# A two-layer network on one core: the last sums of the second layer put into the next pair's turn, its opening run sequence by sequence, and the router's silu computed through the tangent

## The reference, cut to what matters

```
x = x + attn0(cond0(x))
h = cond2_0(x)            # layer norms, an MLP with silu, layer norm
x = x + experts(h)        # softmax router, top 2 of 8, 80 slots per sequence
x = x + attn1(cond1(x))
x = x + ffn1(cond2_1(x))
```

```
out = acc * x_scale * weight_scale + bias      # then added to x
```

## Time and profile before

| | us |
|---|---|
| median of 3 runs | 2380.55 (2374.33 to 2380.96) |
| the profiled execution's own time | 2381.17 |
| its span | 2379.4 |

### The profile page before, as it was taken

How to read it: one execution, slowest core, us unless ns; L and a number is a source line. 1 busy time by engine, 2 the same in 40 slices (tenths; PEclk the granted TensorE clock), 3 DMA queues, 4 the chain that set the end, 5 groups by cost and what they waited for, 6 DMA issues and landing times. The chain is left out here.

```text
span 2379.4 us, 33839 instructions
## 1 busy us (share of the span) xinstructions
PE 2054.9 (86%) x11838; PEld 1300.9 (55%) x11838; DVE 1314.7 (55%) x3682; ACT 1019.4 (43%) x2518; POOL 862.2 (36%) x594
## 2 busy tenths in 40 slices
PE   5588898898898898898898898899999497979897
PEld 4355554554555555555555555567788254545555
DVE  3757577577577577577577544512111255655545
ACT  2244466466465465466466456331222041414141
POOL 1717265365364364364364320411000341515131
PEclk9586999988988988988988889799999698999998
DMA  7000110210210210210210220333454411202000
GB/s 279 36 21 1 52 49 1 92 27 1 92 27 1 92 27 1 92 27 1 92 27 1 81 72 1 125 119 121 150 188 144 143 40 35 56 18 72 18 14 19
DMA packets 67429, 145.89 MB, mean 61 GB/s; under 512 B 16356, under 2 KB 42074, under 8 KB 62946
## 3 DMA queue, kind: packets, MB, share of 16 engines
q1 hardware_dynamic: 51434, 93.79, 11.7%
q0 software_dynamic: 15872, 50.35, 7.3%
HBM read 114.64 MB, written 29.46 MB: 61 GB/s over the span
## 5 line engine op out<-in xcount | busy, mean ns | idle before, releaser
L1386 ACT ACTIVATE att_buf<-att_buf,nmin 128x384 f32<-128x384 f32 (+3 forms) x512 | 288.6, 564 | 402.8 <-DVE nmin L1751 402.6
L1164 PE MATMUL bank<-kk,qT 32*128 32x512 f32 (+2 forms) x1024 | 292.6, 615 | 39.0 <-DVE nmin L1751 38.7
L1197 PE MATMUL bank<-ident,att_buf 128*128 128x128 f32 x1280 | 227.7, 306 | 58.9 <-ACT att_buf L1394 58.2
L901 POOL TENSOR_TENSOR big<-ex_at,kx 128x2048 f32<-128x2048 f32 x56 | 206.8, 3720 | 163.4 <-DVE xt_na L1496 130.1
L1740 DVE TENSOR_TENSOR att_buf<-bank,wdiag 128x128 f32<-128x128 f32 x384 | 93.0, 284 | 241.7 <-PE bank L1169 240.4
L1394 ACT COPY att_buf<-bank 128x384 f32<-128x384 f32 (+3 forms) x512 | 211.0, 412 | 28.7 <-PE bank L1211 27.0
L1211 PE MATMUL bank<-att_buf,vp 128*32 128x128 f32 x2560 | 219.0, 308 | 0.0
L1197 PEld LDWEIGHTS bank<-ident,att_buf 128*128 128x128 f32 x1280 | 158.2, 157 | 79.1 <-ACT att_buf L1386 77.2
L913 POOL DMA_INDIRECT buf_d<-nB,sidx x64 | 62.6, 978 | 358.2 <-DVE sidx L1615 341.1
L1211 PEld LDWEIGHTS bank<-att_buf,vp 128*32 128x32 f32 x2560 | 136.0, 121 | 55.1 <-issue 47.4
L1164 PEld LDWEIGHTS bank<-kk,qT 32*128 32x128 f32 x1024 | 100.5, 205 | 117.5 <-DVE nmin L1751 64.8
(11 more groups left out here) (377 smaller groups left out, 4097.5 us busy)
## 6 DMA issues: line engine op xcount, KB each, us to landing
big<-in_eW SPq DMA_DIRECT2D x16, 1024.0 KB, 7.9
kk<-in_eW SPq DMA_DIRECT2D x16, 1024.0 KB, 7.7
buf_d<-zero SPq DMA_DIRECT2D x8, 640.0 KB, 7.5
xt_na<-in_xT SPq DMA_DIRECT2D x8, 512.0 KB, 3.5
nA<-in_xN SPq DMA_DIRECT2D x8, 512.0 KB, 3.6
x_d<-x SPq DMA_DIRECT2D x8, 512.0 KB, 3.3
x<-x_d SPq DMA_DIRECT2D x8, 512.0 KB, 4.3
out<-qf SPq DMA_DIRECT2D x8, 512.0 KB, 2.9
```

The lines of the kernel that those rows point to most:

```text
L901: pool.tensor_tensor(pv[:, c * P:(c + 1) * P, :].rearrange("p (h d) o -> p o h d", d=DH), spread(ex[:, t, :, 8 * c:8 * c + 8], 3, DH), spr ...
L1164: pe.matmul(bank[u % 2][:, 0:n], qT[r:r + 32, g, i * P:(i + 1) * P], kk[r:r + 32, g, T * i * P:T * i * P + n], start=True, stop=False)
L1197: mm = pe.transpose(bank[3 + u % 2][:, j * P:(j + 1) * P], pr[:, u % NPR, j * P:(j + 1) * P], ident[:])
L1386: act.activation(pr[:, u % NPR, 0:n], pr[:, u % NPR, 0:n], ACT.Exp, scale=-1.0, bias=nmin[:, u % 4:u % 4 + 1], accum_out=rsum[:, i, h:h + ...
```

## The change

1. **Router's activation.** silu(v) = v * (0.5 * tanh(0.5 v) + 0.5) with v = u + b. ScalarE: two `Tanh` with scale 0.5 and bias `half_b`, then two `Identity` with scale 0.5 and bias 0.5 in place. VectorE, at a new step "gate" (unit 26, 27 in the last pass): two `scalar_tensor_tensor` (bank + bias) * aT3, which now raise `u_ok`. VectorE prepares `half` and `half_b` once in each pass.
2. **Last sums of a turn.** `finish` (the same five instructions for each lane) stands at stage `ST_IN` of the next turn; SyncE stores from there. Only the last turn also finishes itself. So that the banks are free, `QK_OUT` becomes (0, 1, 2, 3, 0, 1), and TensorE waits for the lane's four sums before it writes bank 2. GpSimd's new `xb` waits for the lane's finish, and ScalarE's first write to `qf` for the store's landing. `gi` is fetched at the turn's start, and `row_numbers` stands behind kT and k2 on VectorE. Turn 0 is now written out ahead of the loop.
3. **Opening.** TensorE and ScalarE do the whole head of lane 0, then of lane 1. VectorE waits for the two head weights alone, prepares both heads' weights, then does `combine` lane by lane; its preparation of the turn's weights (`wqb`, `orfk`, `orfq`) comes last.

```
-def body(b2, more):
+def finish(dve, v, s, name):
+    for t in range(T):
+        dve.scalar_tensor_tensor(fo[:, t, :], bk[2 + t // 2][...], ab[:, 1, t:t + 1], row("ws"), ALU.mult, ALU.mult).then_inc(s(name + "_raw"), 1)
+    dve.wait_ge(s(name + "_raw"), T)
+    dve.tensor_tensor(fo, fo, v["xb"][:], ALU.add).then_inc(s(name), 1)
+def body(b2, before, more):
...
 sync:
+    if more: fetch_gates(...)            # both lanes, first of all
     brow, wde loads
+    if before: store(..., "fin0", LANES * b2 - LANES + n)
     if more: wait xb_ok; fetch_rows; fetch_head
-    wait fin; store; wait out
+    if not more: store(..., "fin", ...)
...
 gpsimd:
+    if before: pool.wait_ge(s("fin0"), 1)
     pool.tensor_tensor(v["xb"][:], v["x2"], ..., ALU.add)
...
 tensor:
+    if before and i == 2: pe.wait_ge(s("fin0_raw"), T)
...
 vector:
+    if before:
+        yield ST_IN
+        finish(dve, v, s, "fin0")
     yield ST_QK
-    if more: row_numbers(dve, v, s)
     kT, k2
+    if more: row_numbers(dve, v, s)
...
-with nc.Fori(0, B // LANES - 1, hint_back_edge=True) as b2:
-    body(b2, True)
-body(B // LANES - 1, False)
+body(0, False, True)
+with nc.Fori(1, B // LANES - 1, hint_back_edge=True) as b2:
+    body(b2, True, True)
+body(B // LANES - 1, True, False)
```

More of the change, by code:

```diff
@@ L676, in program @@
                 pc3 = sb("pc3", [P, 8])
+                half_b = sb("half_b", [P, K2])
+                half = sb("half", [P, 1])
                 gac = sb("gac", [P, T, 2 * D])
@@ L1325, in router_stream @@
                                     out_of_bank(3)
+                                    yield AT["silu"]
+                                    act.wait_ge(s("half_ok"), 2)
                                     for o in range(K2):
-                                        yield AT["silu"]
                                         act.wait_ge(s("u_mm"), o + 1)
-                                        act.activation(aT3[:, o, :], bank[SIDE[o]][:], ACT.Silu, bias=pc3[:, 6 + o:7 + o]).then_inc(s("u_ok"), 1)
+                                        act.activation(aT3[:, o, :], bank[SIDE[o]][:], ACT.Tanh, bias=half_b[:, o:o + 1], scale=0.5)\
+                                            .then_inc(s("tanh_ok"), 1)
+                                    for o in range(K2):
+                                        act.wait_ge(s("tanh_ok"), o + 1)
+                                        act.activation(aT3[:, o, :], aT3[:, o, :], ACT.Identity, bias=half[:, 0:1], scale=0.5).then_inc(s("gate_ok"), 1)
                                     yield AT["sd3"]
@@ L1553, in router_stream @@
                                     yield from affine(nB, nB[:], gb[:, :, 0:D], gb[:, :, D:2 * D], AT["h2b"], "h_ok")
+                                    yield AT["gate"]
+                                    for o in range(K2):
+                                        dve.wait_ge(s("gate_ok"), o + 1)
+                                        dve.scalar_tensor_tensor(aT3[:, o, :], bank[SIDE[o]][:], pc3[:, 6 + o:7 + o], aT3[:, o, :],
+                                                                 ALU.add, ALU.mult).then_inc(s("u_ok"), 1)
                                     yield AT["y_in"]
@@ L1860, in layer1, with in_stages @@
             lane_bufs.append(v)
-        def in_stages(s, *programs):
-            live = [p(n, lane_bufs[n], lambda name, n=n: s(f"{name}_{n}")) for p in programs for n in range(LANES)]
+        def in_stages(s, *programs, lanes=None):
+            lanes = range(LANES) if lanes is None else lanes
+            live = [p(n, lane_bufs[n], lambda name, n=n: s(f"{name}_{n}")) for p in programs for n in lanes]
             due = [next(g) for g in live]
@@ L2028, in _ @@
                     def _(sp):
+                        if more:
+                            for n, v in enumerate(lane_bufs):
+                                fetch_gates(sp, v, lambda name, n=n: s(f"{name}_{n}"), LANES * b2 + LANES + n)
                         for n, v in enumerate(lane_bufs):
@@ L2039, in _ @@
                                 fetch_head(sp, v, lambda name, n=n: s(f"{name}_{n}"), LANES * b2 + LANES + n)
-                        for n, v in enumerate(lane_bufs):
-                            sp.wait_ge(s(f"fin_{n}"), 1)
-                            sp.dma_start(out[LANES * b2 + n].rearrange("(t p) d -> p t d", p=P), v["fo"]).then_inc(s(f"out_{n}"), 16)
-                        for n in range(LANES):
-                            sp.wait_ge(s(f"out_{n}"), 16)
+                        if before:
+                            for n in range(LANES):
+                                sp.wait_ge(s(f"fin0_out_{n}"), 16)
+                        if not more:
+                            for n, v in enumerate(lane_bufs):
+                                store(sp, v, lambda name, n=n: s(f"{name}_{n}"), "fin", LANES * b2 + n)
+                            for n in range(LANES):
+                                sp.wait_ge(s(f"fin_out_{n}"), 16)
                     @block.gpsimd
@@ L2095, in lane @@
                                     pe.wait_ge(s("ksq_ok"), 2 * (i - 3))
+                                if before and i == 2:
+                                    pe.wait_ge(s("fin0_raw"), T)
                                 for m in range(K2):
@@ L2310, in lane @@
                             dve.wait_ge(s("acc_mm"), 1)
-                            for t in range(T):
-                                done(dve.scalar_tensor_tensor(fo[:, t, :], bk[2 + t // 2][:, (t % 2) * D:(t % 2 + 1) * D], ab[:, 1, t:t + 1],
-                                                              row("ws"), ALU.mult, ALU.mult))
-                            settle()
                             dve.wait_ge(s("x3b_ok"), 1)
-                            dve.tensor_tensor(fo, fo, v["xb"][:], ALU.add).then_inc(s("fin"), 1)
+                            if not more:
+                                finish(dve, v, s, "fin")
                         in_stages(s, lane, *([head_dve(dve)] if more else []))
                 s.clear()
-        with nc.Fori(0, B // LANES - 1, hint_back_edge=True) as b2:
-            body(b2, True)
-        body(B // LANES - 1, False)
+        body(0, False, True)
+        with nc.Fori(1, B // LANES - 1, hint_back_edge=True) as b2:
+            body(b2, True, True)
+        body(B // LANES - 1, True, False)
 def layouts(i):
```

51 lines of the change are left out of this document (37 added, 14 removed).

## The result

The changed kernel took 2303.28 us (median of 4 runs, 2299.39 to 2307.12), the kernel before beside it 2377.44 us: a ratio of 0.969, 95% interval 0.9661 to 0.9719. The rival that came nearest is the one in which the clock comes back too (2315). In every table behind this the medians are over all executions, while the ratios and intervals leave out the slow ones, those over 1.5% above the fastest of their kernel.

A forecast was written before the change was run, and what follows sets the result against it. TensorE's stops and clock were taken to bound the kernel. Router 17.5, last pass -2.0, opening 7.1 and gaps 25.5 summed to 48.1 us off 2381.2, giving 2333.1 profiled and 2332 us forecast; range 2313 to 2353.

The forecast's parts named there:

- the one in which the clock comes back too: Rival: the high clock returns at the router and at the turns, 65.5 us gained, 2315 us; chance 0.15.
- Step 1, the sure part: Router, seven passes: ScalarE free 1.3 us earlier, TensorE's 2.50 us stop becomes 1.2 us; 9 us gained.
- Step 1, the clock: Router, seven passes: shorter stop may keep TensorE's clock up, up to 2.4 us more a pass, half counted.
- The gate at nothing: Router, seven passes: VectorE's two added gates, about 1.65 us, cost nothing; cover is some 1 us.
- Its rival (2350): Router: VectorE's delayed biases give back the 1.3 us and the clock; 2350 us, chance 0.2.
- Step 2: Router, last pass: halvings and gate delay the `wint2` matmuls, 2 us lost, up to 4 with the clock.
- Step 3: Opening: turn 0 starts on TensorE at 1886.7 instead of 1893.83, 7.1 us gained, ends 5 and 9.
- Step 4: Three gaps between turns: stop falls to 2.5 us, 8.5 us a gap, 25.5 us gained, ends 16 and 28.
- The clock behind it, counted at nothing: Turn starts after the shortened gaps: 2.9 us a turn hang on the clock; nothing counted, 9 us as good end.
- The rival in which work comes back inside the turn: Turns: VectorE's sums and later gathers delay TensorE at lane 1's values; 2340 to 2344 us, chance 0.08.

The follow-up runs named there:

- first pair of traces: Profiled executions of the first comparison: the kernel before at 2381.17 us and the changed kernel at 2299.39 us.
- group 3: One chip, the changed kernel and three variants with TensorE's router stop at 0.88, 2.10, 2.50, 2.71 us: 2382.24, 2390.68, 2420.14, 2414.65 us.
- hold 2: Changed kernel plus two unread ScalarE activations behind the halvings in the seven attention passes: 2390.68 us against the changed kernel's 2382.24 in group 3.
- silu passes: Changed kernel with silu back in the seven attention passes, tangent and gate only in the last: 2420.14 us against the changed kernel's 2382.24.
- Silu last: Changed kernel with silu kept in layer 0's last pass only: 2377.49 us against the changed kernel's 2384.88 in group 4; 2355.19 us in group 1.
- group 4: One chip: before 2438.95 us, changed 2384.88, seven passes' halving on VectorE with silu in the last 2356.16, silu last 2377.49, router as before 2423.44.
- the gaps alone: Changed kernel with the last sums and stores put back into their own turn: 2396.62 us against the changed kernel's 2374.3.
- all of layer 1: Changed kernel with the router as before: 2383.09 us against the kernel before's 2402.04 in group 1; ratio 0.9965 in group 4.
- group 1: One chip: before 2402.04 us; changed kernel with router as before 2383.09, router's change alone 2372.08, silu last 2355.19, hold 2 2364.92.
- group 5: One chip: kernel before profiled again, 2370.27 us against 2373.29; changed kernel with seven passes' halving on VectorE and silu in the last, 2292.31 us.
- groups 2 to 4: Follow-ups on one chip each; the first of them had before 2434.92 us, changed 2374.3, three unread activations 2418.06, halving on VectorE 2367.34, sums put back 2396.62.

## Why the prediction was wrong

*What bounds the kernel.* That TensorE's stops and its clock are what counts held everywhere.

*Step 1, the sure part:* right in kind, a little low. ScalarE saved 1.50 us where 1.3 were forecast, since tangents, halvings and the exponential overlap by 0.12 us at each seam; the stop shrank by 1.62. That is 7 x 1.62 = 11.3 us against 9. By the 2.66 us a switch of the Trainium skill ("ScalarE: Activation LUTs", What ACT_TABLE_LOAD costs) two switches would, as an estimate, have been worth 5.3 us, and 4 us after the halvings. The rows show 1.50: two loads of 1.28 us less the halvings' 1.34, and 0.3 us at the seams. The measurement decides, and no drain is in it.

*Step 1, the clock: this is the step that failed.* I had "up to 2.4 us more a pass ... I count half of it", that is 1.2. The first pair of traces has 43.5 / 7 = 6.2 us of busy time a pass, and group 3 has 27 us beyond the stop's length, 3.8 a pass. Two things were wrong. I priced only the matmuls that stand behind the stop, and the clock is lost and won in the whole rest of the pass: of the 43.5 us only 10.5 lie between the first and the last `wint2` matmul. And "Neither row says whether a stop of 1.2 us does so; I count half of it" put a chance into a sum: the rival in which it comes back had 26 us for the router, and its sum of 2315 was the nearest of all. It was near by luck in part: it had half of what the passes gave (26 for 50.7) and 9 us for the clock at the turns, of which little came.

*The gate at nothing:* held. Its rival (2350) fell with it, and its argument from five passes of one length misled: with the stop shorter no pass of the first trace was over 171.3 us.

*Step 2:* sign right, size low. The first trace says 7.4 us. Over all profiled executions the last pass with the experts takes 338.9 us with the gate (mean of 11) and 335.3 with silu (mean of 9): 3.6 us, near the 4 that I gave for the case that the clock goes too. It goes in eight of the 11 (2.90 to 3.63 us instead of 1.99); in the other three, the two of hold 2 and silu passes, the same stop of 2.83 us left it up. Silu last was 7 us faster than the changed kernel in group 4, within the intervals.

*Step 3:* right on this pair, 6.7 against 7.1, and that is half luck, since the opening has two outcomes. Of 17 traces with the changed opening eight have 36.1 to 36.8 us, eight 42.2 to 42.8 and one 40.4; the upper value is nearly the 43.2 to 43.5 of the three with the opening as before. TensorE's up projection of lane 1 and what follows, in the changed kernel and in silu last (group 4), which is the same code here:

```profile
1886.81 1.98 PE L1956 MATMUL bank<-dT,wup 64*128 64x512 f32 x4 [0.68 <-ACT dT L1968]
1891.96 4.60 PE L2147 MATMUL bank<-hcT,wkv 128*128 128x512 f32 x5 [3.17 <-PEq L107]
```

```profile
1872.67 3.78 PE L1964 MATMUL bank<-dT,wup 64*128 64x512 f32 x4 [0.68 <-ACT dT L1976]
1879.64 4.54 PE L2155 MATMUL bank<-hcT,wkv 128*128 128x512 f32 x5 [3.19 <-PEq L107]
```

Lane 1's transposes, down and up projection take 1.10, 1.93 and 1.98 us in the first and 1.97, 3.68 and 3.78 us in the second, 4.4 of the 6 us between the outcomes; over the last 18 us the granted clock is 0.78 in the one and 0.50 in the other. From the last gather to turn 0 it is 13.7 us and 21.1. I had not priced the clock there, though the lanes now stand one behind the other.

*Step 4:* right on this pair, 26.1 against 25.5, and the stop between turns was 2.5 us as reckoned. The clock behind it, counted at nothing, gave little: the first eight records of turns 1 to 3 took 5.39, 6.37 and 5.38 us instead of 6.51, 6.54 and 6.66. On the other chips the gain was smaller: 22 us for the gaps alone, and 19 and 8.5 for all of layer 1. The rival in which work comes back inside the turn was right there in its place but not in its mechanism: what comes back is stops without a releaser and busy time, and not a wait for lane 1's values.

The profiled execution came out 34 us below the sum's 2333.1: the passes (+33, nearly all of it clock) and the 5 us ahead of them, which no part of the change touches, less the 5 of step 2. The median, 4 us above the profiled execution, is 29 us below 2332.

## What to carry to other kernels

When a change shortens a stop of the engine whose clock follows its work, price the clock over the whole stretch around it (here the loop's pass, ahead of the stop too), by the busy time of equal instructions in it, and not by the matmuls right behind the stop; and give the outcome "it comes back" its own case instead of half a term. A series that only lengthens one stop (0.88, 2.10, 2.50, 2.71 us) told in one go what undoing the change could not: whether the table load, the gate or the stop was the cost. And what a gap gives, once it is taken away, can come back inside the stretch that follows (23 us of hand-over, 10 us of time in group 1): read the whole stretch.

## What was not expected of the hardware

- A stop's price can jump: 1.2 us more of it cost 8.4 us in seven passes, 0.4 us more again cost 30. The Trainium skill ("TensorE: Matmul & The Clock Gate", A second HAM failure mode: psum-queue depth-cycling) reports of a bf16 kernel that TensorE's clock swings between its levels where it idles briefly between groups of matmuls, and pays for it in throughput. The traces of this f32 kernel agree: granted clocks of 0.88 to 0.95 over the seven passes, with no stop above 3.8 us in them.
- TensorE has stops with no releaser at fixed places of the program whose length differs from group to group, and so from chip to chip. Near the end of a pass of the first layer they were nil in the first pair and in group 5, 2.2 us in group 1, and 3.7 us in most passes of groups 2 to 4. TensorE, group 3, the changed kernel, third pass, about 9 us before its end:

```profile
801.44 0.63 PE L1213 MATMUL bank<-att_buf,vp 128*32 128x128 f32 x8 [3.69 <-issue]
```

  That such a stop is the arrival of instructions is my guess; no run here shows it.
- Equal passes can fall into step: with silu, pass after pass was 177.5 us long with the same matmuls slow in each, in the first trace and in those of groups 1 and 5, though in group 1 each pass had over 3 us of stops without a releaser that the others lacked. With silu in groups 3 and 4 most were 184 to 188 us.
